# One attention and feed-forward layer on one core: the value projection cut in two and laid among the transposes of the next chunk, products of x with the low-rank factors behind the keys, and a first part of the second group's keys and queries loaded earlier

## The reference, cut to what matters

```python
x = L0_attn_x                          # (2, 1024, 512), fp32
xn = _layernorm(x, axis=-1)
s = _L0_attn_ref(xn, Wq, Wkv, Wo, bo)  # 32 query heads of 16, 8 groups of keys and values, causal
g = _silu(_L0_ffn_ref(xn, ...))        # gate, up and down of width 1376, each with a rank-16 addition
return x + s * g

# in _L0_attn_ref
q = jnp.dot(x, Wq).reshape(b, t, H, HD).transpose(0, 2, 1, 3)
kv = jnp.dot(x, Wkv).reshape(b, t, G, 2, HD).transpose(2, 3, 0, 1, 4)
k, v = (kv[:, 0], kv[:, 1])
k = jnp.broadcast_to(k[:, :, None], (G, b, REP, t, HD)).reshape(b, H, t, HD)
weights = jax.nn.softmax(jnp.where(causal, -jnp.inf, q @ k) / HD ** 0.5)
```

## Time and profile before

| | before |
|---|---|
| time, median of 3 runs | 928.84 us (928.5 to 931.58) |
| profiled execution | 929.51 us, span 927.8 us, mean granted clock 0.988 |
| TensorE busy | 882.7 us, 95% of the span |
| VectorE, ScalarE, GpSimd busy | 574.6, 488.4, 345.2 us (62%, 53%, 37%) |
| longest single wait of TensorE behind the start | 7.0 us, for a DMA of queries (`q<-scratch_q`) |

### The profile page before, as it was taken

How to read it: one execution, slowest core, us unless ns; L and a number is a source line. 1 busy time by engine, 2 the same in 40 slices (tenths; PEclk the granted TensorE clock), 3 DMA queues, 4 the chain that set the end, 5 groups by cost and what they waited for, 6 DMA issues and landing times.

```text
span 927.8 us, 21796 instructions
## 1 busy us (share of the span) xinstructions
PE 882.7 (95%) x8415; PEld 643.3 (69%) x8415; DVE 574.6 (62%) x1674; ACT 488.4 (53%) x1002; POOL 345.2 (37%) x340
## 2 busy tenths in 40 slices
PE   3988699999999999999999999999999999999997
PEld 3764477676767777776767777665677777787885
DVE  6666375766665757565666666677766667651136
ACT  3432365656565656565666565656645454545211
POOL 4152236363635354544445454432121313130133
PEclk9999799999999999999999999998999999999999
DMA  8465525343434343434343535356565546434664
GB/s 279 156 198 167 146 66 145 80 143 82 139 90 133 96 134 97 131 94 128 88 133 78 143 84 146 84 145 184 191 219 158 167 133 194 155 99 137 213 206 136
DMA packets 143094, 129.80 MB, mean 140 GB/s; under 512 B 37360, under 2 KB 115920, under 8 KB 140816
## 3 DMA queue, kind: packets, MB, share of 16 engines
q1 hardware_dynamic: 142992, 128.41, 47.6%
HBM read 74.09 MB, written 53.74 MB: 138 GB/s over the span
## 4 chain that ended last, share of the span: by engine, by line
PE 87%; DVE 4%; DMA 3%; ACT 2%; SPq 2%; issue 2%; DVEq 0%; ACTq 0%
PE bank L1096 27%; PE bank L1140 15%; PE o L1278 14%; PE s L1242 9%; PE st L1261 8%; PE bank L304 3%; PE bank L305 2%; PE bank L306 2%; PE bank L1059 1%; PE bank L1105 1%; DMA scratch_k<-proj_hi 1%; DMA sums<-scratch_o 1%; PE bank L1074 1%; SPq L966 1%; PE s L1249 1%
## 5 line engine op out<-in xcount | busy, mean ns | idle before, releaser
L1543 ACT ACTIVATE prob<-st 128x512 f32<-128x512 f32 (+1 forms) x640 | 323.5, 554 | 260.9 <-PE st L1261 259.5
L1808 DVE CUSTOM_DVE_ANT_0 junk<-s,mask 128x128 bf16<-128x128 f32 (+3 forms) x512 | 229.1, 486 | 80.0 <-PE s L1242 79.4
L1811 DVE TENSOR_REDUCE part_max<-s 128x1 f32<-128x512 f32 x256 | 164.0, 682 | 126.7 <-PE s L1242 126.3
L1242 PE MATMUL s<-k,q 64*128 64x512 f32 (+3 forms) x768 | 157.9, 375 | 15.1 <-DMA q<-scratch_q 7.0
L1096 PE MATMUL bank<-x_hi,w_hi 64*128 64x512 f32 (+1 forms) x704 | 151.7, 414 | 1.3 <-DVE proj_lo L1629 0.8
L602 POOL TENSOR_SCALAR_AFFINE_SELECT prob<-prob 128x512 f32<-128x512 f32 x128 | 80.8, 643 | 181.0 <-ACT prob L1543 180.7
L1278 PE MATMUL o<-prob,v 128*32 128x512 f32 (+3 forms) x1536 | 145.4, 497 | 0.0
L1096 PE MATMUL bank<-x_lo,w_hi 64*128 64x512 f32 (+1 forms) x704 | 144.2, 393 | 0.0
L1096 PE MATMUL bank<-x_hi,w_lo 64*128 64x512 f32 (+1 forms) x704 | 143.6, 391 | 0.0
L1261 PE MATMUL st<-q,k 64*128 64x512 f32 (+3 forms) x768 | 141.9, 345 | 0.2 <-DMA q<-neg_rows 0.2
L1242 PEld LDWEIGHTS s<-k,q 64*128 64x128 f32 x768 | 80.8, 186 | 52.0 <-DVE part_max L1808 22.2
(11 more groups left out here) (156 smaller groups left out, 1175.3 us busy)
## 6 DMA issues: line engine op xcount, KB each, us to landing
late_context_hid_in<-scratch_hid SPq DMA_DIRECT2D x16, 1408.0 KB, 6.9
q<-scratch_q SPq DMA_DIRECT2D x60, 200.0 KB
scratch_hid<-tanh_hid_hi SPq DMA_DIRECT2D x40, 256.0 KB, 2.4
scratch_hid<-hid_lo SPq DMA_DIRECT2D x40, 256.0 KB, 3.0
scratch_o<-o_sb SPq DMA_DIRECT2D x32, 256.0 KB
scratch_q<-proj_hi SPq DMA_DIRECT2D x30, 256.0 KB
k<-scratch_k SPq DMA_DIRECT2D x30, 192.0 KB
x_again<-in_L_attn_x SPq DMA_DIRECT2D x16, 256.0 KB, 5.0
```

What stands on the lines that cost most here:

```text
L1242: pe.matmul(sb_[(p + odd) % S_BANKS][:, 0:wd], q[half, g % 2, h // 2, qt * P:(qt + 1) * P], k[half, g % 2, k0:k0 + wd], start=True, stop=T ...
L1543: nc.scalar.activation(prob[:, job % 3, h, 0:JOB_COLS[j]], st[at % ST_BANKS][:, 0:JOB_COLS[j]], ACT.Exp, scale=float(HD) ** -0.5).then_inc ...
L1808: ins = dve.tensor_tensor_reduce(junk[:, n % S_BANKS, 0:wd], bank_[:, 0:wd], mask[:, C - wd:C], 1.0, LOWEST, ALU.add, ALU.max, part[:, h, ...
L1811: ins = dve.tensor_reduce(part[:, h, qt, dst:dst + 1], bank_[:, 0:wd], AX.X, ALU.max)
```

## The change

The values of a chunk are made in two halves of two token tiles each, `("value", c, 0)` and `("value", c, 1)`, each with its own turn of a bank and its own copy by ScalarE. Chunk 0's halves stay where the values were; the halves of chunk c-1 go behind the first and the second transpose of chunk c. Chunk 3's halves and `low` 1 come behind the keys of chunk 3. Group 1 gets its first loads in `load_second`, issued behind the store of `("proj", 1, 1)`: the first 512 columns of its keys (chunk 2) and all of its queries. Only the later 512 columns of its keys (chunk 3) are still loaded in slot `LOAD`, on a semaphore of their own, `late_keys`, which TensorE waits for at the first unit of the group's second half.

```diff
-STEPS = dict(turn=1, proj=KT, value=TT, low=KT, ...)
+STEPS = dict(turn=1, proj=KT, value=TT // 2, low=KT, ...)
+def turns_and_values(c):
+    for k in range(KT):
+        yield "turn", c, k
+        if k < 2:
+            yield "value", c - 1, k
 def bank_order():
     ...
-    for c in range(2):
-        yield "value", c, 0
+    for n in range(2):
+        yield "value", 0, n
     for c in BESIDE:
-        for k in range(KT):
-            yield "turn", c, k
-        if c == 3:
-            yield "low", 1, 0
+        yield from turns_and_values(c)
         yield ("proj", *BESIDE[c])
         yield "proj", c, KEYS_BLOCK
-        yield "value", c, 0
+    yield "low", 1, 0
+    for n in range(2):
+        yield "value", NCH - 1, n
 ...
+            def load_second():
+                newest = max(projection(0, 0), projection(1, 0), projection(2, KEYS_BLOCK))
+                for a in range(2):
+                    sp.wait_ge(p_stored[a], 3 * DMA * len(range(a, newest + 1, 2)))
+                for h in range(2):
+                    sp.dma_start(k[head_rows(h, ROWS), 1, 0:C].bitcast(F32), k_dram[1][:, 0:C]).then_inc(loaded[1][0], DMA)
+                for h in range(REP):
+                    sp.dma_start(q[head_rows(h, AUG), 1, h // 2].bitcast(F32), q_dram[REP + h]).then_inc(loaded[1][h // 2], DMA)
 ...   (SyncE, background)
                     store_projection(*BESIDE[c])
                     if c == 3:
-                        load_x_a()
+                        load_second()
                     yield STEPS["proj"]
                     store_projection(c, KEYS_BLOCK)
-                    yield STEPS["value"]
-                    store_value(c)
+                yield STEPS["low"]
+                store_x_a(1)
+                yield STEPS["value"]
+                load_x_a()
+                yield STEPS["value"]
+                store_value(NCH - 1)
 ...   (SyncE, attention)
-                        cols = slice(0, T) if g else slice(C, T)
+                        cols = slice(0, T) if g >= 2 else slice(C, T)
                         for h in range(2):
                             sp.dma_start(k[head_rows(h, ROWS), g % 2, cols].bitcast(F32), k_dram[g][:, cols])\
-                                .then_inc(loaded[g % 2][0], DMA)
-                        for h in range(REP):
+                                .then_inc(late_keys if g == 1 else loaded[g % 2][0], DMA)
+                        if g != 1:
+                            for h in range(REP):
 ...   (TensorE)
-            def value(c):
+            def value(c, n):
                 pe.wait_ge(xT_copied, KT * (c + 1))
-                out_ = take_bank(("value", c, 0))
-                for t in range(TT):
+                out_ = take_bank(("value", c, n))
+                for t in range(n * TT // 2, (n + 1) * TT // 2):
 ...
+                if g == 1 and w == NU_A:
+                    pe.wait_ge(late_keys, 2 * DMA)
 ...   (ScalarE)
             def copy_x(c, kt):
                 if c >= 2:
-                    wait_filled(act, ("value", c - 2, 0))
+                    wait_filled(act, ("value", c - 2, 1))
 ...
-            def copy_value(c):
-                key = ("value", c, 0)
+            def copy_value(c, n):
+                key = ("value", c, n)
+                tiles = slice(n * TT // 2, (n + 1) * TT // 2)
```

More of the change, by code:

```diff
@@ L120 @@
 FOLD_STEPS = [2] * (NH - 2) + [1] * 2
-STEPS = dict(turn=1, proj=KT, value=TT, low=KT, hidden=2 * KT, down=NH + 1, out=KT)
+STEPS = dict(turn=1, proj=KT, value=TT // 2, low=KT, hidden=2 * KT, down=NH + 1, out=KT)
 SPLIT_DOWN, SPLIT_OUT = 12, NT // 2
@@ L535, in read_out @@
                 return (gate_read, NCH * a + b + 1), (up_read, NCH * a + b + 1)
-            return dict(turn=(xT_copied if a else xT_lo, KT * a + b + 1), proj=(p_lo, (kind == "proj" and projection(a, b)) + 1), value=(v_copied, a + 1),
+            return dict(turn=(xT_copied if a else xT_lo, KT * a + b + 1), proj=(p_lo, (kind == "proj" and projection(a, b)) + 1), value=(v_copied, 2 * a + b + 1),
                         low=(x_a_lo, a + 1), down_fold=(d_lo, a + 1), down=(y_done, a + 1),
@@ L667, in background @@
                 low_query_weights(3)
-                yield NUMBER_STEPS["value", NCH - 1, 0] - done
-                done = NUMBER_STEPS["value", NCH - 1, 0]
+                yield NUMBER_STEPS["value", NCH - 1, 1] - done
+                done = NUMBER_STEPS["value", NCH - 1, 1]
                 for i in range(2):
@@ L849, in background @@
                 store_x_a(0)
-                for c in range(2):
-                    yield STEPS["value"]
-                    store_value(c)
+                yield 2 * STEPS["value"]
+                store_value(0)
                 for c in BESIDE:
-                    yield KT * STEPS["turn"]
+                    yield KT * STEPS["turn"] + 2 * STEPS["value"]
+                    store_value(c - 1)
                     for n in range(4 * (c - 2), 4 * (c - 2) + 4):
                         load_raw(n)
-                    if c == 3:
-                        yield STEPS["low"]
-                        store_x_a(1)
                     yield STEPS["proj"]
@@ L1194, in background @@
                 yield from low(0)
-                for c in range(2):
-                    yield from value(c)
+                for n in range(2):
+                    yield from value(0, n)
                 for c in BESIDE:
[L1198 to L1201, removed]
+                    for kind, chunk, n in turns_and_values(c):
+                        yield from (turn_x if kind == "turn" else value)(chunk, n)
                     yield from project(*BESIDE[c])
                     yield from project(c, KEYS_BLOCK)
-                    yield from value(c)
+                yield from low(1)
+                for n in range(2):
+                    yield from value(NCH - 1, n)
                 for c, blk in AFTER[:SOON]:
@@ L1365, in round_weight @@
                 if n == 0:
[L1366 removed]
+                    wait_filled(act, ("value", NCH - 1, 1))
                     act.wait_ge(xT_lo_late, 2 * KT)
@@ L1449, in background @@
                 round_x_a(0)
-                for c in range(2):
+                for n in range(2):
                     yield STEPS["value"]
-                    if c:
-                        root(3)
-                    copy_value(c)
+                    copy_value(0, n)
+                root(3)
                 for c in BESIDE:
[L1456 to L1462, removed]
+                    for kind, chunk, n in turns_and_values(c):
+                        yield STEPS[kind]
+                        if kind == "turn":
+                            round_x(chunk, n)
+                            copy_x(chunk, n)
+                        else:
+                            copy_value(chunk, n)
                     yield STEPS["proj"]
@@ L1466, in background @@
                     split_projection(c, KEYS_BLOCK)
+                yield STEPS["low"]
+                round_x_a(1)
+                for n in range(2):
                     yield STEPS["value"]
-                    copy_value(c)
+                    copy_value(NCH - 1, n)
                 for i in range(2):
@@ L1739, in background @@
                     low_projection(c, KEYS_BLOCK)
-                    yield STEPS["value"]
+                yield STEPS["low"]
+                low_of_x_a(1)
+                yield 2 * STEPS["value"]
                 for c, blk in AFTER[:SOON]:
```

19 lines of the change are left out of this document (9 added, 10 removed).

## The result

| | before | changed |
|---|---|---|
| median of the runs | 928.5 us (7 runs, 924.54 to 931.58) | 921.73 us (7 runs, 919.73 to 923.63) |
| ratio, 95% interval | | 0.9931 (0.9906 to 0.9957) |
| profiled execution, span | 929.51, 927.8 us | 919.73, 917.9 us |
| TensorE busy | 882.7 us (95%) | 879.1 us (96%) |
| mean granted clock | 0.988 | 0.992 |

A second measurement, beside experiments 2 to 4, gave 920.8 us against 928.58, a ratio of 0.9913 (0.9893 to 0.9934). So the change gains 6.8 to 7.8 us, 0.7 to 0.9%; I had forecast 10.85 us and 918.0 us, in a range of 915.2 to 922.5. The two profiled executions lie 9.8 us apart (before's is a little above its median, the changed one is the fastest of its runs); 0.7 us of that is the start, where the first transpose begins at 12.44 us instead of 13.10.

The account below looks back on a forecast made before the run. TensorE, busy 882.7 us or 95% of the span, was taken to bound the kernel. Terms 7.0 + 2.4 + 1.3 + 0.1 - 0.15 + 0.2 = 10.85 us gave 918.0 us, range 915.2 to 922.5.

Parts of the forecast that it names:

- The loads of group 1: TensorE's 7.04 us wait for group 1's queries goes whole, loads issued at about 79 us; late keys wanted later.
- rival D: SyncE stands at load_x_a for low-rank stores, delaying late keys, last values, rows of maxima: 7.9 us lost; chance 0.03.
- The clock behind it: Half clock from 100.5 to 110.5 us, behind the wait for group 1, becomes full clock: 2.4 us gained.
- The transposes of chunk 2: Chunk 1's value work moves in, hardly any idle to fill: 0.1 us gained, within 0.3 either way.
- The transposes of chunk 3: Value work hides ScalarE's copies, idle falls from 1.67 to 0.4 us: 1.3 us gained.
- The keys of chunk 2: TensorE waits earlier, for the keys' split, which ends sooner as GpSimd's chain starts 0.5 us sooner: -0.15 us.
- rival A: Half clock from 62.5 to 66.5 us goes too, worth 1.7 us more, 916.3 us; chance 0.15.
- The maxima: Three waits beside chunk 3's projections fall from 1.91 to 1.7 us: 0.2 us gained.
- Rival B: low_x, loaded behind the low-rank products, or another next consumer comes late past a 3 us margin: 920 to 923 us; chance 0.18.
- Given back later: Sign of a wrong forecast: TensorE's waits beyond 130 us grow by more than 1 us in sum.

Follow-up runs that it names:

- experiment 2: Kernel before with only the early loads of group 1 (load_second, late_keys), the order of values, low-rank products and transposes unchanged: 926.35 us, 0.9978.
- experiment 3: Changed kernel without load_second and late_keys, group 1 loaded in one piece in its old slot: 927.69 us, 0.9996.
- experiment 4: Changed kernel with GpSimd's first x_lo of chunk 2 held until VectorE has normalised chunk 3: 918.22 us, 0.99.
- experiment 7: Experiment 4 with low 1 between chunk 3's queries and keys, its store ahead of load_second: 917.92 us, 0.9888.
- experiment 8: Experiment 7 with the edits of experiment 5 and experiment 6 added: 915.28 us, 0.9857.
- experiment 1: The changed kernel measured once more with no edit: 920.8 us, 0.9913.
- experiment 6: Changed kernel with GpSimd's low_b pair moved behind the last split of query weights: 918.41 us, 0.9892.
- experiment 5: Experiment 2 with group 1's slot load (late keys) moved from slot 1 to 8, behind the rows of maxima: 919.44 us, 0.9904.

## Why the prediction was right in direction and range, and too large

Step by step, in the profile (the times are of one execution each; I compare distances, so the 0.7 us of the start is out):

- **The loads of group 1, 7.0 us: right in size, and by luck of the order.** The wait went whole, the loads were issued at 79.99 (79 forecast). But my sentence that the late keys are not wanted for long is about TensorE, and what decided was SyncE's queue: alone, the same loads turn the 7.04 us into 6.61 us at `st`. I had named that place in rival D, and had priced it by the low-rank store only.
- **The clock behind it, 2.4 us: right.** From the first unit of group 1 to the first use of `low_x` it was 112.83 - 105.14 = 7.69 us; it is 103.86 - 98.58 = 5.28 us, 2.41 less.
- **The transposes of chunk 2, +0.1 us: wrong, -2.5 us.** This is the step that failed, and it makes up the whole gap between the 10.85 us forecast and the 8.3 us of the sum below. From the first transpose to the query projection of chunk 2 there are now 52.06 - 12.44 = 39.62 us. Before it was 37.1 (first transpose 13.10, projection 50.23). I had counted what ScalarE gets and had not followed `x_lo` to GpSimd, which starts 5.5 us sooner there (42.70 instead of 48.20) and falls on VectorE's normalisation of chunk 3. The price is 1.66 us of wait, 0.25 at the end, and half clock from 47 to 51. Experiment 4 shows it by its removal. The runs also show how firm the number is. The stretch took 37.2 to 37.6 us where GpSimd was kept off (experiments 4, 7 and 8), 39.6 to 40.6 with the wait and half clock behind it (changed kernel, experiments 1 and 3), and 38.2 with the same wait and full clock (experiment 6). So the hold itself costs under 1 us and the half clock, which does not come every time, 1.4 to 2.4. With the order of before it took 37.1, 36.4 and 36.0 us (before, experiments 2 and 5), so the -2.5 is good to about 1 us. For the same reason group 1 began at 98.58 and not at 96 to 97.
  I had cited the section of the Trainium skill that bears on this (SBUF — State Buffer, "Who interferes with whom"), but only what it says of operations with two SBUF inputs, and had applied that at one place. The section also names `cast` and `tensor_scalar` among the VectorE operations that can take the port pair shared with GpSimd. The traces agree: `TENSOR_SCALAR` 3.84 us against 1.92, `CAST` 2.85 us against 0.17.
- **The transposes of chunk 3, +1.3 us: two thirds.** The waits for copies fell from 1.67 to 0.83 us (0.4 expected), as the fourth transpose covered only 0.45 us of the copies of the third, not 0.6, and TensorE started 0.15 us after the last copy's end; some of the stretch ran at half clock.
- **The keys of chunk 2, -0.15 us: the mechanism right, the size a little off.** GpSimd's pair of `low_b` ended at 62.25, 1.79 us behind the start of TensorE's transpose at 60.46; before, it ended 2.25 us behind the start of the values (60.91 - 58.66), so it came 0.5 us sooner, as forecast. But the idle is 2.19 us (1.8 expected). This time the cast was held (59.44, 2.85 us, to 62.29) and not the last step, which came behind it, so the split ended 0.85 us after GpSimd instead of 0.64; and TensorE started 0.15 us after the split's end (63.10), which I had not counted. The half clock stayed, so rival A did not come in the changed kernel.
- **The maxima, +0.2 us: right.** 0.77 + 0.47 + 0.58 = 1.82 us, expected 1.7, before 1.91.
- **Rival B** (0.18) did not strike in the changed kernel, but its margin was thinner than my 3 us: the low-rank store took 5.1 us to land (median), not 2.9. In experiment 4, with TensorE 3.7 us ahead at the first use of `low_x` and a landing of 8.8 us for the later transfer, it struck. In experiment 6, 4.0 us ahead (99.89) but with a landing of 6.8 us, the load went at 92.11 and TensorE did not wait. So the landing decides as much as TensorE's lead; why it took 2 us longer in experiment 4 is open.
- **Given back later: no.** TensorE's waits beyond 130 us sum to 10.1 us in the changed kernel and 9.9 before.

The sum as measured, by the places of the two profiles: +7.0, +2.4, -2.5, and about +1.4 for the stretch from the query projection of chunk 2 to where TensorE is ready for group 1; 8.3 us up to L1105, distances from the first transpose. My three terms for that stretch add to the same 1.35 us (1.3 - 0.15 + 0.2), in part by luck: the named waits there fell by 0.43 us only (5.27 to 4.84), and what made the rest is open. My lower end of the gain was added up wrongly: by my own bounds it is about 5.0 us, not 5.4. The rest of the profiles' 9.9 us is the start (0.7) and 0.9 us spread over the 800 us behind, which I can't put to a cause. The medians (6.8 and 7.8 us) are near the 8.3.

## What to carry to other kernels

A load that is moved forward must be followed in the queue that issues it: look at what stands behind each wait of that queue, not only at who wants the data. Work moved forward on TensorE moves its followers on all engines; look for the VectorE operations with which GpSimd's will now coincide. And two edits that are nothing or little alone can be worth much together, so a part is judged with the rest in place.

## What the runs showed of the hardware that I had not expected

- GpSimd's `x_lo` (two SBUF inputs, 1.26 us) doubles the time of VectorE's normalising operations that run beside it: four `TENSOR_SCALAR` of 128x512 took 3.84 us with it and 1.92 us without. Small operations are held as well: a cast of 128x16 took 2.85 us beside GpSimd's `low_b`, which it outlasted by 0.04 us, and 0.17 us without.
- A store of 256 KB took 13.4 us from its issue to its landing behind 992 KB of loads of group 1, 768 KB of `low_x` and two stores like it (experiment 2), and 8.09 us without the first of these. The low-rank store (median of its two transfers) took 2.4 to 3.7 us to land where no early loads were ahead of it (before, experiments 2, 3, 5, 7 and 8), and 5.1, 6.8 and 6.0 us behind them (the changed kernel, experiments 4 and 6).
- Idle of TensorE of 1.5 to 2.2 us was followed by half clock in some executions and not in others, and its length does not tell which. One and the same wait, of 1.66 or 1.67 us in the transposes of chunk 2, had half clock behind it in the changed kernel and in experiments 1 and 3, and full clock in experiment 6. Waits of 1.48 us (experiment 4, before 60.90) and of 2.08 us (experiment 5, before 57.74) had full clock behind them; waits of 1.69 us (before), 1.96 us (experiment 7) and 2.19 us (the changed kernel) had half. I have no experiment that tells what decides.
